# A softmax attention stage on one core: ACT's exponentials of the second pair's first head, moved to the front of the double turn

## The chip, the cores and the metric

The kernel runs on one NeuronCore of a Trainium2 chip. Its engines are TensorE (PE; PEld is its weight load), VectorE (DVE), ScalarE (ACT), GpSimd (POOL) and SyncE (SP, which only issues DMAs here). Each runs its own list of instructions in order, and they meet at semaphores. The metric is the device time of one execution in microseconds, lower being better. Three runs of the kernel before took 1304.85, 1305.89 and 1306.28 us; the median is 1305.89 us.

## The reference

The input x has shape (32, 256, 128), in float32. Six residual blocks follow each other, each on a layer norm of x: three products with a tanh, a linear attention, the tanh block again, a spectral product (folded into one circulant matrix), a causal softmax attention with 16 heads, and the spectral product again. The change touches only the softmax attention:

```python
q = jnp.einsum('qdh,bcd->bhcq', Q, x) * sq
k = jnp.einsum('qdh,bcd->bhcq', K, x) * sq
v = jnp.einsum('vdh,bcd->bhcv', V, x) * sv
att = jnp.einsum('bhcq,bhCq->bhcC', q, k) / d_query
causal = jnp.arange(T)[:, None] >= jnp.arange(T)[None, :]
att = jnp.where(causal, att, -jnp.inf)
p = jax.nn.softmax(att, axis=-1)
y = jnp.einsum('bhcC,bhCv->bhcv', p, v)
z = jnp.einsum('dvh,bhcv->bcd', W, y) * (math.sqrt(d_embed / d_value) / num_heads)
```

## The kernel before

x stays in SBUF for the whole program. Four phases (FFN, linear attention, FFN, spectral) go over 16 groups of two batches. Then comes the softmax stage, from about 267 us to the end: 32 batches, each in 8 turns p = 0 to 7, one turn per pair of heads (n = 8b + p). PE and POOL are written by turns. DVE and ACT are written by double turns: p = 0, 2, 4, 6, each with the pairs n and n+1. Below, "turn 6" of ACT means this double turn. The order on every engine is fixed by the order of the calls in its `batch` function. The first two and the last two batches are written out, the others run in a loop of two.

For a pair, PE computes q and k (`qk_product`, six products into one PSUM bank, L1058 to L1060). ACT copies the bank of an even pair out (`qk_whole`, L749, into `qk_raw`, semaphore `qk_out`), which frees the bank for the next odd pair. ACT then casts the high part (`qk_high_even` L755, `qk_high_odd` L761), and DVE computes the low part (`qk_low`, L506). PE computes the scores of two heads (`scores`, L1073), with those of pairs n+2 and n+3 one behind the other in the odd turn. DVE masks them and takes row maxima (`mask_scores`, L520). ACT takes the exponentials with their sums (`exp_head`, L776, one call per head: a 128x128 and a 128x256 ACTIVATE, each with a read of the sum). DVE inverts the sums (L528), POOL scales (`scale_probs`, L326 and L328, semaphore `pn_ready`), PE transposes (`probs_transpose`, L1087), DVE and ACT copy the transposes to `pT` (L535, L785), and PE multiplies with the values (`products`, L1104). The results of two pairs lie in one bank, from which ACT copies y to the ring `space` (`y_out`, L802, semaphore `y_ready`).

Between these, PE has other work by turn. Turns 0 and 1 hold values of this batch, turn 2 the transposes of x (L1050) and of the spectral part (L1121), turns 3 to 5 the output projection of the last batch (L1113) and the spectral product (L1129), and turns 6 and 7 values of the next batch (L1093 to L1095). ACT copies the values out (`values_out`, L793) in turns 0 and 6.

Three of PE's waits concern what ACT delivers around the change:

```python
pe.wait_ge(exp_ready, count(2 * n - 2))                               # L1067, scores
pe.wait_ge(y_ready, count(y_calls))                                   # L1085, fifth of six transposes
pe.wait_ge(qk_out, count(b * (PAIRS // 2) + (p // 2 + 2)))            # L1159, odd qk_product
```

The first means that the scores of pair n+3 wait until both heads of pair n+1 have gone through the exponential, since they take the same PSUM banks. `X_TURN` is 2, and PAIRS is 8. The buffers `pr` are three: even pairs use buffer 0, odd pairs 1 and 2 in turn.

Of the kernel before, what the change touches and what calls it, by code (L numbers as in the profile page):

```python
# [54 lines left out]
def count(n):  # L55

    return n.i * n.step + n.base if isinstance(n, Count) else n
# [49 lines left out]
def above_0(n):  # L107

    return isinstance(n, Count) or n > 0


def build(nc, x, Wq, bq, Wd, bd, Wu, bu, Wo, bo, W1, W2, W3, ffn_bias, Q, K, V, W, w_re, w_im, fft_bias, dft, out):
    ctx = ExitStack()
    with ctx:
# [128 lines left out]
        X_TURN, LN_TURN, W_TURN, V_TURN, Z_TURN = 2, 4, 3, 6, 6  # L243

        def pr_of(p):

            return 0 if p % 2 == 0 else 1 + p % PAIRS // 2 % 2
# [389 lines left out]
        def _(act):  # L637
# [101 lines left out]
            def x_high(b, j):  # L739
                act.wait_ge(tr_done, count(b + (SOFT + 1)))  # L740
                if above_0(2 * PAIRS * (b - 1)):
                    act.wait_ge(s_done, count(2 * PAIRS * (b - 1)))
                nc.scalar.copy(x_hi[:, j, :], ps[:, BANK_X, 0:T]).then_inc(xhi_ready, 1)

            def qk_whole(n):
                act.wait_ge(qk_done, count(n + 1))
                if above_0(n - 1):
                    act.wait_ge(qklo_ready, count(n - 1))
                nc.scalar.copy(qk_raw[:], ps[:, BANK_QK, :]).then_inc(qk_out, 1)  # L749

            def qk_high_even(n, evens):
                act.wait_ge(qk_out, count(evens))
                if above_0(2 * n - 2):
                    act.wait_ge(s_done, count(2 * n - 2))
                nc.scalar.copy(qk_hi[:, 0].rearrange("p s k -> p (s k)"), qk_raw[:]).then_inc(qkhi_ready, 1)  # L755

            def qk_high_odd(n):
                act.wait_ge(qk_done, count(n + 1))
                if above_0(2 * n - 2):
                    act.wait_ge(s_done, count(2 * n - 2))  # L760
                nc.scalar.copy(qk_hi[:, 1].rearrange("p s k -> p (s k)"), ps[:, BANK_QK, :]).then_inc(qkhi_ready, 1)  # L761

            def exp_head(n, j, h, buf):

                act.wait_ge(max_ready, count(2 * n + (1 + h)))
                if h == 0:
                    kept = n - 1 if buf == 0 else n - 3
                    if above_0(kept):
                        act.wait_ge(pt_done, count(kept))
                    if above_0(n - 1):  # L770
                        act.wait_ge(rinv_ready, count(n - 1))
                for qt in range(2):
                    w = (qt + 1) * P
                    at = 2 * h + qt
                    dst = pr[:, buf, h, 0, :] if qt == 0 else pr[:, buf, h, 1:3, :].rearrange("p b k -> p (b k)")
                    last = nc.scalar.activation(dst, ps[:, BANK_S + 2 * j + h, qt * P:qt * P + w], ACT.Exp,  # L776
                                                bias=neg_max[:, j, at:at + 1], scale=-1.0, accum_out=rsum[:, j, at:at + 1])
                last.then_inc(exp_ready, 1)

            def probs_T(n, j):  # L780

                act.wait_ge(pt_done, count(n + 1))
                if above_0(n - 1):
                    act.wait_ge(pv_done, count(n - 1))
                nc.scalar.copy(pT[:, j].rearrange("p h b q -> p (h b q)")[:, 512:768], ps[:, BANK_Y, j * T:(j + 1) * T]).then_inc(pTb_ready, 1)  # L785

            def values_out(b, j, c, bank=BANK_X):

                act.wait_ge(v_done, count(4 * b + (c + 1)))
                if c == 0:  # L790
                    if above_0(PAIRS * (b - 1)):
                        act.wait_ge(pv_done, count(PAIRS * (b - 1)))
                nc.scalar.copy(vv[:, j, c % 2, 512 * (c // 2):512 * (c // 2) + 512], ps[:, bank, :]).then_inc(v_ready, 1)  # L793

            def y_out(b, jb, p, first=False):

                act.wait_ge(pv_done, count(b * PAIRS + p))
                if p == 1 and above_0(b - 1):
                    act.wait_ge(w_done, count(b - 1))
                at = jb * PAIRS + p - 1  # L800
                if at > 0:
                    nc.scalar.copy(y_ring[:, (at - 1) * T:(at + 1) * T], ps[:, BANK_Y, :]).then_inc(y_ready, 1)  # L802
                else:
                    if not first:
                        nc.scalar.copy(yT[:, 1, PAIRS - 1, :], ps[:, BANK_Y, 0:T])
                    nc.scalar.copy(yT[:, 0, 0, :], ps[:, BANK_Y, T:2 * T]).then_inc(y_ready, 1)
# [5 lines left out]
            def z_xT_out(b, w_after=None):  # L812
                act.wait_ge(z_tr_done, count(b + 1))
                if above_0(b):
                    act.wait_ge(w_done, count(b + 1 if w_after is None else w_after))
                nc.scalar.copy(z_xT[:], ps[:, BANK_X, T:2 * T]).then_inc(z_xT_ready, 1)
# [13 lines left out]
            def batch(b, jb, first=False, last=False):  # L830
                for p in range(0, PAIRS, 2):
                    n = b * PAIRS + p
                    if p > 0:
                        y_out(b, jb, p - 1, first)
                    elif not first:
                        y_out(b - 1, 1 - jb, PAIRS - 1)
                    if not (last and p == PAIRS - 2):
                        qk_whole(n + 2)
                    if p == 0:
                        values_out(b, jb, 2)  # L840
                    if p == X_TURN and above_0(b - 1):
                        z_xT_out(b - 2)
                    if p == X_TURN and not last:
                        x_high(b + 1, 1 - jb)
                    if p == V_TURN and not last:
                        values_out(b + 1, 1 - jb, 0)
                    if not (last and p == PAIRS - 2):
                        qk_high_even(n + 2, b * (PAIRS // 2) + (p // 2 + 2))
                    exp_head(n + 1, 1, 0, pr_of(p + 1))
                    if not (first and p == 0):  # L850
                        probs_T(n - 1, 1)
                    if not (last and p == PAIRS - 2):
                        qk_high_odd(n + 3)
                    exp_head(n + 1, 1, 1, pr_of(p + 1))
                    if p == 0:
                        values_out(b, jb, 3)
                    if p == V_TURN and not last:
                        values_out(b + 1, 1 - jb, 1)
                    probs_T(n, 0)
                    if not (last and p == PAIRS - 2):  # L860
                        exp_head(n + 2, 0, 0, 0)
                        exp_head(n + 2, 0, 1, 0)

            batches(act, batch)
            y_out(B - 1, 1, PAIRS - 1)
            z_xT_out(B - 2)
# [378 lines left out]
```

## Time and profile before

| what | value |
|---|---|
| median of 3 runs | 1305.89 us |
| the profiled execution's own time | 1308.45 us |
| its span (first to last instruction) | 1306.7 us |
| PE matmul busy | 1245.7 us, 95% |
| PE weight load busy | 1072.3 us, 82% |
| DVE busy | 1028.3 us, 79% |
| ACT busy | 1006.9 us, 77% |
| POOL busy | 589.8 us, 45% |
| mean granted TensorE clock | 0.990 |

The busy shares are means over the whole program. The chain that ended last runs over PE for 88% of the span. In a matmul line of the timeline, the distance between two starts tells more than the duration, because matmuls overlap. A wait in brackets names the engine and line that ended it. Waits under 0.17 us are not shown in brackets and have to be read from distances between starts.

### The profile page before, as it was taken

Reading aid. Unit: us, or ns where it says so; the run is one execution under the profiler, and the core shown is the slowest. Engines: PE = TensorE matmul, PEld = TensorE weight load, DVE = VectorE, ACT = ScalarE, POOL = GpSimd, SP = SyncE. Lnnn points to the kernel's source line nnn. Section 1 sums busy time; section 2 is a strip of 40 time slices with the busy share of each in tenths; the row PEclk is TensorE's granted clock in tenths of the full one; section 3 lists DMA queues with packets and bytes.
Section 4 is the critical chain, followed back from the end, with each engine's and each line's share of the span. In section 5 each row is a group of like instructions: output and inputs, shape, how many; then the busy total and the mean of one; then the engine's idle time right before and its main releaser. Section 6 shows DMA issues by size and latency. Waiting matters only on the chain.

```text
span 1306.7 us, 38948 instructions
## 1 busy us (share of the span) xinstructions
PE 1245.7 (95%) x11323; PEld 1072.3 (82%) x11331; DVE 1028.3 (79%) x4813; ACT 1006.9 (77%) x3393; POOL 589.8 (45%) x913
## 2 busy tenths in 40 slices
PE   5799987799999999999999999999999999999997
PEld 4688876778788888888888888888888888888885
DVE  6877779977778787778787878788787878787774
ACT  4744448578788888888888888888888888888883
POOL 5811138634344444444444444444444444444443
PEclk9999989989999999999999999999999999999999
DMA  8000000000000000000000000000000000000000
GB/s 215 1 1 0 1 1 1 1 2 2 3 3 9 8 0 8 0 8 0 8 0 8 0 8 0 8 0 8 0 8 0 8 0 8 0 8 0 9 2 18
DMA packets 14303, 11.83 MB, mean 9 GB/s; under 512 B 709, under 2 KB 12522, under 8 KB 14058
## 3 DMA queue, kind: packets, MB, share of 16 engines
q1 hardware_dynamic: 14240, 11.19, 3.2%
q8 instruction: 24, 0.39, 0.1%
q14 instruction: 29, 0.24, 0.1%
q10 hardware_dynamic: 10, 0.00, 0.0%
HBM read 7.00 MB, written 4.19 MB: 9 GB/s over the span
## 4 chain that ended last, share of the span: by engine, by line
PE 88%; DVE 4%; issue 3%; POOL 2%; ACT 2%; DMA 1%; SPq 1%; DVEq 0%; POOLq 0%; ACTq 0%
PE ps L1073 16%; PE ps L1104 14%; PE ps L1087 13%; PE ps L1113 9%; PE ps L1058 6%; PE ps L1059 5%; PE ps L1060 5%; PE ps L1095 2%; PE ps L1094 2%; PE ps L1093 2%; PE ps L987 2%; PE ps L945 1%; PE ps L1005 1%; PE ps L1035 1%; PE ps L1129 1%
## 5 line engine op out<-in xcount | busy, mean ns | idle before, releaser
L776 ACT ACTIVATE pr<-ps,neg_max 128x128 f32<-128x128 f32 (+1 forms) x1024 | 425.9, 431 | 118.6 <-DVE neg_max L520 118.6
L326 POOL TENSOR_TENSOR pr<-pr,rinv 128x256 f32<-128x256 f32 x256 | 157.9, 617 | 555.9 <-DVE rinv L528 555.9
L520 DVE CUSTOM_DVE_ANT_0 ps<-ps,mask 128x128 f32<-128x128 f32 (+1 forms) x1024 | 329.2, 389 | 3.3
L328 POOL TENSOR_TENSOR pr<-pr,rinv 128x512 f32<-128x512 f32 x256 | 266.6, 1041 | 0.0
L535 DVE COPY pT<-ps 128x512 f32<-128x512 f32 x256 | 175.4, 685 | 100.9 <-PE ps L1087 100.9
L776 ACT ACTIVATION_READ_ACCUMULATOR pr<-ps,neg_max 128x1 f32 x1024 | 219.0, 214 | 0.0
L1087 PE MATMUL ps<-ident,pr 128*128 128x128 f32 x1536 | 210.2, 273 | 2.4 <-POOL pr L328 1.1
L1087 PEld LDWEIGHTS ps<-ident,pr 128*128 128x128 f32 x1536 | 179.1, 141 | 21.4 <-POOL pr L328 2.4
L1104 PE MATMUL ps<-pT,space 128*64 128x256 f32 (+1 forms) x2048 | 194.9, 332 | 0.7 <-ACT pT L785 0.5
L1104 PEld LDWEIGHTS ps<-pT,space 128*64 128x64 f32 x2048 | 126.8, 136 | 55.0 <-ACT pT L785 0.7
L1058 PE MATMUL ps<-x_hi,wqk_hi 128*128 128x256 f32 x512 | 168.1, 328 | 3.0 <-issue 2.6
L1073 PE MATMUL ps<-qk_hi 64*128 64x128 f32 (+1 forms) x1024 | 162.9, 313 | 1.6 <-DVE qk_lo L506 0.5
L1059 PE MATMUL ps<-x_lo,wqk_hi 128*128 128x256 f32 x512 | 144.4, 282 | 0.0
L1060 PE MATMUL ps<-x_hi,wqk_lo 128*128 128x256 f32 x512 | 144.0, 281 | 0.0
L1073 PE MATMUL ps<-qk_lo,qk_hi 64*128 64x128 f32 (+1 forms) x1024 | 143.1, 274 | 0.0
L1073 PE MATMUL ps<-qk_hi,qk_lo 64*128 64x128 f32 (+1 forms) x1024 | 142.7, 274 | 0.0
L520 DVE DVE_READ_ACCUMULATOR2_ANT neg_max<- 128x1 f32 x1024 | 142.0, 139 | 0.0
L1113 PE MATMUL ps<-wz,space 128*128 128x128 f32 x1024 | 132.7, 278 | 0.6 <-ACT space L810 0.6
L506 DVE TENSOR_TENSOR qk_lo<-ps,qk_hi 128x512 fp32r<-128x512 f32 x128 | 88.5, 692 | 51.2 <-ACT qk_hi L761 47.6
L1073 PEld LDWEIGHTS ps<-qk_hi 64*128 64x128 f32 x1024 | 97.7, 186 | 34.8 <-issue 21.1
L1113 PEld LDWEIGHTS ps<-wz,space 128*128 128x128 f32 x1024 | 122.1, 191 | 3.8 <-issue 0.8
L1058 PEld LDWEIGHTS ps<-x_hi,wqk_hi 128*128 128x128 f32 x512 | 96.6, 189 | 26.1 <-issue 24.2
(171 smaller groups left out, 2582.5 us busy)
## 6 DMA issues: line engine op xcount, KB each, us to landing
out<-x_all SPq DMA_DIRECT2D x16, 256.0 KB, 2.3
x_all<-L_attn_x SPq DMA_DIRECT2D x1, 768.0 KB, 6.1
x_all<-L_attn_x SPq DMA_DIRECT2D x1, 512.0 KB, 4.0
space<-L_attn_Q SPq DMA_DIRECT2D x1, 512.0 KB, 15.6
space<-L_attn_K SPq DMA_DIRECT2D x1, 512.0 KB, 9.8
space<-L_attn_V SPq DMA_DIRECT2D x1, 512.0 KB, 11.6
space<-L_attn_W SPq DMA_DIRECT2D x1, 512.0 KB, 11.9
dft_s<-dft SPq DMA_DIRECT2D x1, 192.0 KB, 2.6
```

The source lines that it names most:

```text
L326: nc.gpsimd.tensor_tensor(pr[:, buf, :, 0, :], pr[:, buf, :, 0, :], r[:, :, 0:1].to_broadcast([P, 2, P]), ALU.mult)
L328: nc.gpsimd.tensor_tensor(pr[:, buf, :, 1:3, :].rearrange("p h b k -> p h (b k)"), pr[:, buf, :, 1:3, :].rearrange("p h b k -> p h (b k)") ...
L520: last = nc.vector.tensor_tensor_reduce(o, o, mask[:, T - w:T], -1.0, -MASKED, ALU.add, ALU.min, neg_max[:, j, 2 * h + qt:2 * h + qt + 1])
L535: nc.vector.tensor_copy(pT[:, j].rearrange("p h b q -> p (h b q)")[:, 0:512], ps[:, BANK_T, :]).then_inc(pTa_ready, 1)
L776: last = nc.scalar.activation(dst, ps[:, BANK_S + 2 * j + h, qt * P:qt * P + w], ACT.Exp, bias=neg_max[:, j, at:at + 1], scale=-1.0, accum ...
L1058: mm(o, wqk_hi[:, s, of_pair], x_hi[:, jb, :], start=True, stop=False, skip_group_check=True)
L1059: mm(o, wqk_hi[:, s, of_pair], x_lo[:, jb, :], start=False, stop=False, skip_group_check=True)
L1060: last = mm(o, wqk_lo[:, s, of_pair], x_hi[:, jb, :], start=False, stop=True, skip_group_check=True)
L1073: last = mm(ps[:, BANK_S + 2 * j + h, qt * P:qt * P + w], q[of_head, j, 0, qt * P:(qt + 1) * P], key[of_head, j, 1, 0:w], start=(k == 0), ...
L1087: last = tr(to, pr[:, buf, k // 3, k % 3, :], ident[:])
L1104: last = mm(ps[k * DV:(k + 1) * DV, BANK_Y, half * T + kt * P:(half + 1) * T], vv[:, jb, kt, h * DV:(h + 1) * DV], pT[:, j, k, 0:2, :] if ...
L1113: last = mm(ps[:, BANK_X, t * D:(t + 1) * D], yT[:, j, p, t * P:(t + 1) * P], wz[:, p, :], start=(p == 0), stop=(p == PAIRS - 1), skip_gro ...
```

## The change

In the double turns 0, 4 and 6, ACT calls `exp_head` for the first head of pair n+1 as the first thing of the turn, directly behind the two heads of pair n, which close the turn before. Until now it stood behind the copy of y, the copy of `qk_raw`, the values copy (in turns 0 and 6) and the cast `qk_hi`. In turn 2 it stays there. The second head stays where it was in all turns. No instruction is added or removed.

```diff
             def batch(b, jb, first=False, last=False):
                 for p in range(0, PAIRS, 2):
                     n = b * PAIRS + p
+                    if p != X_TURN:
+                        exp_head(n + 1, 1, 0, pr_of(p + 1))
                     if p > 0:
                         y_out(b, jb, p - 1, first)
                     elif not first:
@@ -846,7 +848,8 @@
                         values_out(b + 1, 1 - jb, 0)
                     if not (last and p == PAIRS - 2):
                         qk_high_even(n + 2, b * (PAIRS // 2) + (p // 2 + 2))
-                    exp_head(n + 1, 1, 0, pr_of(p + 1))
+                    if p == X_TURN:
+                        exp_head(n + 1, 1, 0, pr_of(p + 1))
                     if not (first and p == 0):
                         probs_T(n - 1, 1)
                     if not (last and p == PAIRS - 2):
```

ACT's rows of a turn 6 before the change, up to the second head; `space` in L802 is the ring of y, and in L793 it is the values:

```order
L802 COPY space<-ps 128x512 [waits pv_done]
L749 COPY qk_raw<-ps 128x512 [waits qklo_ready,qk_done]
L793 COPY space<-ps 128x512 [waits v_done]
L755 CAST qk_hi<-qk_raw 128x512 [waits s_done,qk_out]
L776 ACTIVATE pr,rsum<-ps,neg_max 128x128 [waits rinv_ready,pt_done,max_ready]
L776 ACTIVATE pr,rsum<-ps,neg_max 128x256
L785 COPY pT<-ps 128x256 [waits pv_done,pt_done]
L761 CAST qk_hi<-ps 128x512 [waits s_done,qk_done]
L776 ACTIVATE pr,rsum<-ps,neg_max 128x128 [waits max_ready]
```

The same turn of ACT after the change:

```order
L776 ACTIVATE pr,rsum<-ps,neg_max 128x128 [waits rinv_ready,pt_done,max_ready]
L776 ACTIVATE pr,rsum<-ps,neg_max 128x256
L802 COPY space<-ps 128x512 [waits pv_done]
L749 COPY qk_raw<-ps 128x512 [waits qklo_ready,qk_done]
L793 COPY space<-ps 128x512 [waits v_done]
L755 CAST qk_hi<-qk_raw 128x512 [waits s_done,qk_out]
L785 COPY pT<-ps 128x256 [waits pv_done,pt_done]
L761 CAST qk_hi<-ps 128x512 [waits s_done,qk_done]
L776 ACTIVATE pr,rsum<-ps,neg_max 128x128 [waits max_ready]
```

The two ACTIVATEs of the first head have moved in front of four other instructions. L785 and everything behind it has the same work in front of it as before.

In turn 4, which has no values copy, ACT's rows before the change are:

```order
L802 COPY space<-ps 128x512 [waits pv_done]
L749 COPY qk_raw<-ps 128x512 [waits qklo_ready,qk_done]
L755 CAST qk_hi<-qk_raw 128x512 [waits s_done,qk_out]
L776 ACTIVATE pr,rsum<-ps,neg_max 128x128 [waits rinv_ready,pt_done,max_ready]
L776 ACTIVATE pr,rsum<-ps,neg_max 128x256
```

and after it:

```order
L776 ACTIVATE pr,rsum<-ps,neg_max 128x128 [waits rinv_ready,pt_done,max_ready]
L776 ACTIVATE pr,rsum<-ps,neg_max 128x256
L802 COPY space<-ps 128x512 [waits pv_done]
L749 COPY qk_raw<-ps 128x512 [waits qklo_ready,qk_done]
L755 CAST qk_hi<-qk_raw 128x512 [waits s_done,qk_out]
```

Here they pass three instructions. The lists of PE, DVE and POOL are the same before and after.

## Rows read from the trace of the kernel before

**Rows 1.** Window over the softmax stage: us; busy us (instructions) of PE, PEld, DVE, ACT, POOL; clock; DMA
```profile
340.00:1290.00 950.00, 947.21 (x9204) 820.75 (x9204) 757.88 (x3622) 796.61 (x2818) 434.33 (x593) 1.00 0.01 4
```

**Rows 2.** Waits, 340 to 1300 us: who for whom, us in total, times, longest
```profile
PEld ps L1073 <- ACT pr L776: 10.6, 56, 0.3
```

**Rows 3.** Timeline of ACT, turn 6: start, us, instruction, [idle before]
```profile
808.08 0.60 ACT L802 COPY space<-ps 128x512 f32<-128x512 f32 x1
808.75 0.59 ACT L749 COPY qk_raw<-ps 128x512 f32<-128x512 f32 x1
809.44 0.59 ACT L793 COPY space<-ps 128x512 f32<-128x512 f32 x1
809.92 0.63 ACT L755 CAST qk_hi<-qk_raw 128x512 fp32r<-128x512 f32 x1
810.45 0.37 ACT L776 ACTIVATE pr<-ps,neg_max 128x128 f32<-128x128 f32 x1
...
811.25 0.38 ACT L785 COPY pT<-ps 128x256 f32<-128x256 f32 x1
811.50 0.61 ACT L761 CAST qk_hi<-ps 128x512 fp32r<-128x512 f32 x1
...
812.69 0.24 ACT L776 ACTIVATION_READ_ACCUMULATOR pr<-ps,neg_max 128x1 f32 x1
```

**Rows 4.** Timeline of PE, the same turn
```profile
807.73 0.39 PE L1058 MATMUL ps<-x_hi,wqk_hi 128*128 128x256 f32 x1
...
809.24 0.82 PE L1087 MATMUL ps<-ident,pr 128*128 128x128 f32 x6
809.82 0.37 PE L1058 MATMUL ps<-x_hi,wqk_hi 128*128 128x256 f32 x1
...
812.07 0.33 PE L1073 MATMUL ps<-qk_hi 64*128 64x128 f32 x2
...
812.98 0.33 PE L1073 MATMUL ps<-qk_hi 64*128 64x128 f32 x2
```

**Rows 5.** Timeline of PE, turn 2: the scores of the two pairs
```profile
827.75 0.33 PE L1073 MATMUL ps<-qk_hi 64*128 64x128 f32 x2
...
828.54 0.22 PE L1073 MATMUL ps<-qk_hi 64*128 64x128 f32 x2
```

**Rows 6.** Timeline of ACT and PE, turn 0
```profile
815.81 0.60 ACT L802 COPY space<-ps 128x512 f32<-128x512 f32 x1
...
816.33 0.59 ACT L749 COPY qk_raw<-ps 128x512 f32<-128x512 f32 x1
...
817.40 0.36 PE L1058 MATMUL ps<-x_hi,wqk_hi 128*128 128x256 f32 x1
```

**Rows 7.** Timeline of DVE, turns 6, 0 and 2
```profile
807.57 0.14 DVE L520 DVE_READ_ACCUMULATOR2_ANT neg_max<- 128x1 f32 x1
...
810.71 0.68 DVE L506 TENSOR_TENSOR qk_lo<-qk_raw,qk_hi 128x512 fp32r<-128x512 f32 x1
...
813.45 0.29 DVE L520 CUSTOM_DVE_ANT_0 ps<-ps,mask 128x128 f32<-128x128 f32 x1
...
821.02 0.29 DVE L520 CUSTOM_DVE_ANT_0 ps<-ps,mask 128x128 f32<-128x128 f32 x1
...
828.75 0.29 DVE L520 CUSTOM_DVE_ANT_0 ps<-ps,mask 128x128 f32<-128x128 f32 x1
```

**Rows 8.** Timeline of ACT and PE, turn 4
```profile
831.12 0.60 ACT L802 COPY space<-ps 128x512 f32<-128x512 f32 x1
...
833.50 0.37 PE L1058 MATMUL ps<-x_hi,wqk_hi 128*128 128x256 f32 x1
```

**Rows 9.** Timeline of PE, batch 0, turn 0
```profile
276.43 0.39 PE L1058 MATMUL ps<-x_hi,wqk_hi 128*128 128x256 f32 x1 [0.34 <-ACT qk_raw L749]
```

**Rows 10.** Timeline of PE, last batch, turn 6
```profile
1286.50 0.41 PE L1087 MATMUL ps<-ident,pr 128*128 128x128 f32 x2 [0.56 <-ACT space L802]
...
1287.84 0.87 PE L1087 MATMUL ps<-ident,pr 128*128 128x128 f32 x6 [0.93 <-POOL pr L328]
```

## Prediction

> **What bounds the kernel now.** I read the softmax stage first, because the edit touches nothing else. One window over 950 us of it [rows 1] shows the matmul side of TensorE (PE) busy for 947.21 us at a granted clock of 1.00, while ACT is busy for 797 us and VectorE (DVE) for 758 us. So the end of this stage is set by PE's instruction stream. ACT's order matters only at the places where PE waits for ACT.
>
> The Trainium skill, "Perfetto Trace Analysis", section Identifying the Most-Contended Engine, warns against exactly this reading: matmul busy time flatters PE, and the busy share of the weight loads should be taken instead. By that rule PE would stand at 820.75 of 950 us [rows 1], 86%, and would have slack in which neither a later nor an earlier ACT result counts, so the sum below would be zero instead of +8.5 us. The trace does not settle this by a busy share; the distances between starts in [rows 4, 5] speak against the rule here.
>
> The second view is the list of waits. Inside the stage PE waits for ACT in one place that repeats: the weight load of the score products (L1073) waits for `pr` (the exponentials), 56 times, 10.6 us in all [rows 2]. In the timeline each of these is a gap in front of the scores of the *second* pair. In turns 6 and 0 the first pair's scores start at 812.07 and the second's at 812.98, 0.91 us later [rows 4]; in turn 2, where nobody is late, the same distance is 828.54 - 827.75 = 0.79 us [rows 5]. So PE loses 0.12 us per such turn, and what it waits for is the second head of pair n+1: its last read ends at 812.69 + 0.24 = 812.93, and PE starts 0.05 us later [rows 3, 4]. I use this 0.05 us for every hand-over from ACT to PE or DVE. The 56 waits are two in nearly every batch, in turns 6 and 0.
>
> **The change, turn by turn.** Nothing is added or removed. One `exp_head` (two ACTIVATEs with their reads) goes from behind the casts to the front of the turn. Its cost on ACT is read from the same rows: 811.25 - 810.45 = 0.80 us from its start to the start of what follows. So the copies of y, of `qk_raw` and, where they exist, the values copy and `qk_hi` come up to 0.80 us later; from `probs_T` on ACT has done the same work as before. No DMA is issued by ACT in the loop and PE, DVE and POOL keep their order. Two of the late results are wanted by PE: `y_ready` in front of the fifth transpose (L1085), and `qk_out` in front of the odd pair's `qk_product` (L1159).
>
> *Can the exponentials start that early?* In turn 6 ACT is free at 808.08, and DVE's maxima for this head end at 807.57 + 0.14 = 807.71 [rows 3, 7]. Yes, with 0.37 us to spare; so the edit does what it says.
>
> *Turn 6, the new wait.* Exponentials 808.08 to 808.88. The y copy then starts at 808.88 and lasts 0.60, so `y_ready` comes at 808.88 + 0.60 + 0.05 = 809.53. PE's transposes start at 809.24 and take (809.82 - 809.24)/6 = 0.097 each, so the fifth wants it at 809.63: just in time, 0.1 us of slack. One copy behind another starts 0.52 us after it (816.33 - 815.81 [rows 6]), so `qk_raw` starts at 809.40 and ends at 809.99. Before, it started at 808.75, held back by PE, so 0.07 us of the 0.80 is idle time that gets used. PE wants to start the odd `qk_product` at 809.82 [rows 4]; it now starts at 809.99 + 0.05 = 810.04: a wait of 0.22 us, to which I add 0.02 us because the first weight load is then no longer under the transposes (the first product after a wait takes 0.39 instead of 0.37 us, [rows 9] against [rows 4]). **Cost 0.24 us.**
>
> *Turn 6, the old wait.* ACT goes on: values 809.88, `qk_hi` 810.36 (0.48 us after the values copy, as 809.92 - 809.44), `probs_T` 810.89 (0.53 later, as 810.45 - 809.92), odd `qk_hi` 811.14 (0.25 later). Its input arrives 1.02 us after the products start, as in 808.75 - 807.73 [rows 3, 4], that is at 811.06. So it starts 0.36 us earlier than before (811.50) and the second head ends at 812.57. PE's second scores start at 812.07 + 0.24 + 0.79 = 813.10 and no longer wait for it. They would have started at 812.98. **Gain 0.12 us, net +0.12 us.** Here the edit pays 0.24 to get back 0.12.
>
> *DVE in turn 6.* Its first `qk_lo` moves from 810.71 to 810.98 + 0.05 = 811.03, the two normalisations behind it keep their place and their 0.6 us, the second `qk_lo` therefore ends at about 812.8, before PE's 813.10. The `pT` copy and the masks follow at about 813.43, as before (813.45 [rows 7]). So ACT gets its next maxima at the same time as before and turn 0 begins on ACT as in the trace, while PE begins it 0.12 us late.
>
> *Turn 0.* The same sum from 815.81 [rows 6]: exponentials to 816.61, y copy to 817.21, `qk_raw` 817.13 to 817.72, PE starts at 817.77 + 0.02 instead of 817.40, so +0.38 against the trace, of which 0.12 was carried in: cost 0.25 or so. The second head ends well before the scores, so the 0.12 us gap goes again: net +0.12 us. The first scores come 2.25 us after the odd `qk_product` (812.07 - 809.82), at 820.04, and the mask of the next pairs 1.00 us after these, as 828.75 - 827.75 in turn 2 [rows 5, 7]: 821.04, against 821.02 in the trace. ACT's next exponentials are not pushed.
>
> *Turn 2* is not edited. PE comes 0.24 us late, ACT's `qk_raw` waits for PE and is late by the same, and everything moves together. *Turn 4*: the y copy starts at 831.12 [rows 8] and would start at 831.92; `qk_raw` would end at 833.03, and PE wants it at 833.50. The project-out matmuls hide the 0.80 us, and there was no gap to win: zero. If that cover were gone it would cost up to 0.8 us per batch.
>
> **Sum.** 61 steady turns (turn 6 of batches 1 to 30, turn 0 of batches 1 to 31) by 0.12 us: +7.3 us. Batch 0 is leaner on PE: in its turn 0 PE already waits for `qk_raw`, 0.34 us [rows 9], so there the full 0.80 us lands. Part of it is given back at the second scores and part is absorbed while PE waits for DVE in turn 2; I estimate +0.6 us for the batch, between 0 and 1.5. In the last turn 6 PE waits for the y copy, 0.56 us [rows 10]; that copy is 0.80 us later, the transposes' end, the `pT` copies and the last head follow, and the next transposes (1287.84) start some 0.65 us later. Everything after is one chain: +0.65, between 0 and 0.8. Together +8.5 us. The profiled execution took 1308.45 us (span 1306.7), so it would take 1317.0; the shown runs have a median 2.6 us lower, so the same 8.5 us gives **1314.4 us**.
>
> Bounds: the unseen term is the wait for `qk_out` in a busy turn. From the restart cost at nothing and a copy that hands over 0.02 us sooner, 0.08 us net a turn: 61 x 0.08 = 4.9 us and the ends at about 0.6, 1311.4. From one more 0.05 us a turn (the tight `y_ready`, or the masks), 0.17: 10.4 us and the ends at 2.3, 1318.6. I take 0.12, the value the rows give.
>
> **The rivals.**
> 1. *The gap closes and nothing opens: faster.* Place: the second scores in turns 6 and 0. Price: 61 x 0.12 = 7.4 us, so 1298.5. It decides if `qk_raw` is ready before PE's 809.77, that is if ACT's delay stays under 0.43 us. For it: the 10.6 us of waits are real [rows 2], and ACT idles for 153 of 950 us [rows 1]. Against it: that idle time does not lie here; the exponentials, the y copy and `qk_raw` stand back to back in front of PE's wait and end 0.65 us late [rows 3].
> 2. *Hidden: no change.* The new wait is no longer than the old one, or PE has slack that matmul records do not show. Then 0 to +2.6 us, about 1307. For it: both terms are 0.1 to 0.2 us, near the resolution of such sums. Against it: turn 2 shows that without a wait the distance is 0.79 and not 0.91, so PE's stream does respond to 0.12 us.
> 3. *The old gap stays.* DVE's `qk_lo`, 0.3 us later, becomes what the second scores wait for, and 0.24 us a turn is paid in full: 61 x 0.24 + 1.3 = 15.9 us, 1321.8. Against it: it ends at 812.8 and is wanted at 813.05.
>
> **How the numbers follow.** Forecast 0.68, rival 1 0.11, rival 2 0.13, rival 3 0.08. The forecast's own range is 1311.4 to 1318.6. To hold 8 in 10 I reach down through the hidden case and a little above: 1305 to 1319. A change of 0.2%, 2.6 us, is what these runs can tell from none. Faster by more: 0.11. Within: rival 2 and a thin tail of the forecast, 0.14. Slower by more: 0.75.
>
> **What would show it.** In the new profile: PE's odd `qk_product` (L1058 behind L1087) with an idle time of about 0.2 us, released by ACT's `qk_raw`, some 61 times, 10 to 15 us in all; no more waits of L1073 for `pr` in turns 6 and 0, so distances of 0.79 there; batches 0.24 us longer (turns 6 and 0 by 0.12 each, turns 2 and 4 unchanged). Wrong in rival 1's way would be no wait for `qk_raw`; in rival 3's, a wait of L1073 for `qk_lo`; and if turn 4 grew, the cover by project-out was misread.

## The result, and the profile after

Eleven runs of the changed kernel have a median of 1311.18 us, eleven runs of the kernel before taken with them 1306.78 us. The ratio is 1.0028, with a 95% interval of 1.0015 to 1.0041, which is +3.7 us (+2.0 to +5.4). So the change makes the kernel a little slower, in the direction of the forecast, but by less than half of the 8.5 us that were forecast.

The profiled execution took 1311.18 us, its span 1309.4 us. First the window over the softmax stage, to be read against [rows 1], with the same columns: PE is as full as before, and ACT has no more work.

```profile
340.00:1290.00 950.00, 947.74 (x9189) 817.24 (x9188) 761.17 (x3618) 784.66 (x2811) 433.12 (x592) 1.00 0.01 4
```

Then the list of waits of the changed kernel, 340 to 1310 us (who waited for whom, us in total, times, longest). PE's lines have moved down by three, so L1061 is `qk_product` and L1076 the scores.

```profile
PEld ps L1061 <- ACT qk_raw L749: 11.9, 58, 0.2
DVE qk_lo L506 <- ACT qk_hi L755: 9.9, 45, 0.2
```

The wait of the scores for `pr` [rows 2] has gone completely. In its place PE waits for `qk_raw`, 58 times, 11.9 us. This is what the forecast asked for as its sign: some 61 times, 10 to 15 us. DVE, too, now waits for the later cast `qk_hi`; before, that cast (L755) does not stand in the list.

The timeline of PE in a turn 6 after the change, to be read against [rows 4]:

```profile
807.54 0.39 PE L1061 MATMUL ps<-x_hi,wqk_hi 128*128 128x256 f32 x1
...
809.05 0.82 PE L1090 MATMUL ps<-ident,pr 128*128 128x128 f32 x6
809.82 0.39 PE L1061 MATMUL ps<-x_hi,wqk_hi 128*128 128x256 f32 x1
...
812.07 0.33 PE L1076 MATMUL ps<-qk_hi 64*128 64x128 f32 x2
...
812.87 0.23 PE L1076 MATMUL ps<-qk_hi 64*128 64x128 f32 x2
...
813.65 1.52 PE L1107 MATMUL ps<-pT,space 128*64 128x256 f32 x16
...
815.10 0.39 PE L1061 MATMUL ps<-x_hi,wqk_hi 128*128 128x256 f32 x1
...
817.52 0.39 PE L1061 MATMUL ps<-x_hi,wqk_hi 128*128 128x256 f32 x1
...
822.80 0.39 PE L1061 MATMUL ps<-x_hi,wqk_hi 128*128 128x256 f32 x1
```

Subtract the turn's start. The odd `qk_product` starts at 2.28 us, 0.19 later than before (809.82 - 807.73 = 2.09). The second scores start 0.80 us after the first. The products (L1107) start 813.65 - 812.87 = 0.78 us after the second scores. The turn is 7.56 us long, against 7.59 before. The last three rows are the turn 0 that follows: its odd `qk_product` starts at 2.42 us (817.52 - 815.10), against 2.08 before, and it is 7.70 us long (822.80 - 815.10). ACT's part of the turn 6, to be read against [rows 3]:

```profile
807.88 0.38 ACT L776 ACTIVATE pr<-ps,neg_max 128x128 f32<-128x128 f32 x1
...
808.67 0.61 ACT L802 COPY space<-ps 128x512 f32<-128x512 f32 x1
809.13 0.63 ACT L749 COPY qk_raw<-ps 128x512 f32<-128x512 f32 x1
```

The copy of `qk_raw` ends at 809.76, and PE starts 0.06 us later.

The starts of PE's `qk_product`, taken from the timeline for all 32 batches, give the length of every double turn. In the loop they repeat to 0.02 us. Before the change, turns 0 and 2 come in two kinds, in odd and even batches; why, I did not look into. The table has the steady length, and the sums over the program, in us:

| | before | after | difference |
|---|---|---|---|
| turn 6, steady | 7.58 | 7.57 | -0.01 |
| turn 0, steady, odd and even batches | 7.58, 7.66 | 7.70, 7.70 | +0.12, +0.04 |
| turn 2, steady, odd and even batches | 7.88, 7.93 | 7.88, 7.88 | +0.01, -0.04 |
| turn 4, steady | 8.75 | 8.75 | 0 |
| sum of 31 turns 6 | 238.01 | 237.81 | -0.20 |
| sum of 32 turns 0 | 243.27 | 247.14 | +3.87 |
| of these, batch 0 | 6.90 | 7.43 | +0.53 |
| of these, batch 2 | 7.67 | 8.71 | +1.04 |
| sums of turns 2 and 4, but for the last turn 4 | 520.82 | 520.79 | -0.03 |
| of these, turn 2 of batch 30 | 7.87 | 8.13 | +0.26 |
| before the first turn | 274.43 | 271.63 | -2.80 |
| start of the last turn 4 to PE's last instruction | 26.82 | 28.72 | +1.90 |

In turn 2 of batch 30 PE now waits 0.2 us for DVE's `x_lo` (L500), a wait that is not in the list of before.

The 2.80 us ahead of the softmax stage lie in code that the change does not touch. The start of the first turn varied between 270.75 and 275.80 us over the eleven profiles of this study, so this is scatter, and it hides part of the loss in this one execution. Two other entries hold more than the waits: in the turn 0 of batch 2 and at the end PE's clock was low for some us. They come below.

### The profile page after: what moved, and what is told of

It is laid out like the page before. It is cut to its first block, busy times and chain, and to the rows that moved or that the text cites. A ratio compares the mean times of both kernels' runs of the same rounds, so it can differ in the third digit from the quotient of the medians.

```text
span 1309.4 us, 38956 instructions
## 1 busy us (share of the span) xinstructions
PE 1248.0 (95%) x11331; PEld 1069.8 (82%) x11331; DVE 1033.7 (79%) x4813; ACT 995.8 (76%) x3393; POOL 589.2 (45%) x913
## 4 chain that ended last, share of the span: by engine, by line
PE 90%; DVE 3%; issue 3%; ACT 2%; DMA 1%; SPq 1%; POOL 0%; DVEq 0%; POOLq 0%; ACTq 0%
PE ps L1076 15%; PE ps L1107 14%; PE ps L1090 13%; PE ps L1116 9%; PE ps L1061 8%; PE ps L1062 5%; PE ps L1063 5%; PE ps L1098 2%; PE ps L1096 2%; PE ps L1097 2%; PE ps L948 2%; PE ps L970 2%; PE ps L990 2%; PE ps L1008 1%; PE ps L1038 1%
## 5 line engine op out<-in xcount | busy, mean ns | idle before, releaser
L776 ACT ACTIVATION_READ_ACCUMULATOR pr<-ps,neg_max 128x1 f32 x1024 | 222.0, 217 | 0.0
L1090 PE MATMUL ps<-ident,pr 128*128 128x128 f32 x1536 | 213.7, 273 | 3.2 <-ACT space L802 1.9
L1107 PE MATMUL ps<-pT,space 128*64 128x256 f32 (+1 forms) x2048 | 196.1, 334 | 0.7 <-ACT pT L785 0.5
L1061 PE MATMUL ps<-x_hi,wqk_hi 128*128 128x256 f32 x512 | 169.6, 331 | 3.9 <-issue 2.8
L1107 PEld LDWEIGHTS ps<-pT,space 128*64 128x64 f32 x2048 | 127.4, 137 | 55.4 <-ACT pT L785 0.7
L1076 PE MATMUL ps<-qk_hi 64*128 64x128 f32 (+1 forms) x1024 | 157.0, 301 | 0.6 <-DVE qk_lo L506 0.5
L1076 PE MATMUL ps<-qk_lo,qk_hi 64*128 64x128 f32 (+1 forms) x1024 | 143.4, 275 | 0.0
L1076 PE MATMUL ps<-qk_hi,qk_lo 64*128 64x128 f32 (+1 forms) x1024 | 143.2, 274 | 0.0
L1061 PEld LDWEIGHTS ps<-x_hi,wqk_hi 128*128 128x128 f32 x512 | 96.5, 188 | 39.7 <-issue 24.4
L785 ACT COPY pT<-ps 128x256 f32<-128x256 f32 x256 | 104.3, 408 | 24.6 <-PE ps L1090 20.6
L1076 PEld LDWEIGHTS ps<-qk_hi 64*128 64x128 f32 x1024 | 97.7, 186 | 22.5 <-issue 21.1
```

The lines of the kernel that those rows point to most:

```text
L1061: mm(o, wqk_hi[:, s, of_pair], x_hi[:, jb, :], start=True, stop=False, skip_group_check=True)
L1076: last = mm(ps[:, BANK_S + 2 * j + h, qt * P:qt * P + w], q[of_head, j, 0, qt * P:(qt + 1) * P], key[of_head, j, 1, 0:w], start=(k == 0), ...
L1090: last = tr(to, pr[:, buf, k // 3, k % 3, :], ident[:])
L1107: last = mm(ps[k * DV:(k + 1) * DV, BANK_Y, half * T + kt * P:(half + 1) * T], vv[:, jb, kt, h * DV:(h + 1) * DV], pT[:, j, k, 0:2, :] if ...
```

## The experiments

Each edit is shown against the kernel before, unless it says otherwise. "Theory B" in the expectations is the sum of the prediction. "Theory A" was made after the result was seen: the new wait costs what the sum said or a little less, but closing the old gap gives back about 0.23 us a turn, 0.12 in front of the second scores and 0.11 inside them.

**Turn 6 alone.**

```diff
+                    if p in (6,):
+                        exp_head(n + 1, 1, 0, pr_of(p + 1))
...
-                    exp_head(n + 1, 1, 0, pr_of(p + 1))
+                    if p not in (6,):
+                        exp_head(n + 1, 1, 0, pr_of(p + 1))
```

> The first head goes to the front in turn 6 alone. Theory A (the new one): the wait for qk_raw costs about 0.19 us there, and closing the gap before the second scores gives back 0.23 us, 0.12 in front of them and 0.11 inside them, so turn 6 gets 0.02 to 0.04 us shorter than the 7.58 us of before: 31 turns, about -1 us in the stage, but the last turn 6 costs up to 1.9 us at the end, together 0 to +1 us. Theory B (the sum on record): 0.24 against 0.12, turn 6 gets 0.12 us longer, +3.7 us in the stage and +0.65 at the end.

Measured: ratio 1.0013 (1.0004 to 1.0023), +1.7 us. The steady turn 6 is 7.57 us instead of 7.58 and the 31 turns sum to 237.63 us, 0.38 less than before; turn 0 is as before. Theory A holds in the stage: in turn 6 the exchange is even. What is lost sits at the end of the program: from the start of the last turn 4 to PE's last instruction it took 29.64 us in this profile, 2.82 more than before (more on it below).

**Turn 0 alone.** The same edit with `(0,)`.

> The first head goes to the front in turn 0 alone. Theory A: the wait for qk_raw costs 0.34 to 0.37 us, since PE starts this turn on time, and the gap gives back 0.23, so turn 0 gets 0.11 to 0.14 us longer, +3.5 to +4.5 us over 32 turns, and nothing at the end. Theory B would have 0.37 against 0.12, +0.25 us a turn when it isn't preceded by a late turn 6, +7.7 us.

Measured: ratio 1.0021 (1.0012 to 1.0030), +2.7 us. The steady turn 0 is 7.72 to 7.73 us, with the odd `qk_product` at 2.44 us instead of 2.08; the 32 turns sum to 247.88 us, +4.6, of which 1.2 are the one turn in batch 2. The loss of the change is in turn 0.

**Turn 4 alone.** The same edit with `(4,)`.

> The first head goes to the front in turn 4 alone. Both theories: PE is busy with the output projection until long after qk_raw is there and has no gap before the second scores, so turn 4 stays at 8.75 us and the whole at 0 within 1 us; only in batch 0, where there is no projection, turn 4 may cost 0.1 to 0.5 us. A rival: half the cost of the change sits here, +2 us.

Measured: ratio 1.0004 (0.9995 to 1.0013). Steady turn 4 is 8.75 us, as before, and in batch 0 it is 7.25 instead of 7.11. The output projection does hide the 0.80 us, and batch 0, which has none, loses only 0.14. The rival falls.

**The gap by itself.** ACT is given time in front of the second head without anything being put in front of `qk_raw`. In the loop's batches this kernel leaves out most of the values that two of the four copies deliver, so it only measures time.

```diff
-                nc.scalar.copy(vv[:, j, c % 2, 512 * (c // 2):512 * (c // 2) + 512], ps[:, bank, :]).then_inc(v_ready, 1)
+                wv = 64 if (isinstance(b, Count) and c % 2 == 0) else 512
+                nc.scalar.copy(vv[:, j, c % 2, 512 * (c // 2):512 * (c // 2) + wv], ps[:, bank, 0:wv]).then_inc(v_ready, 1)
```

> The kernel before, with ACT's values copy of the first and third part narrowed from 512 to 64 columns in batches 2 to 29 and a little beyond (so most of the values are stale). ACT gets some 0.3 us of lead before the second head in turns 6 and 0, nothing is put in front of qk_raw, and PE's list is the same. It measures the gap by itself. Theory A: 0.23 us a turn, turns 6 and 0 at 7.35 to 7.36 us instead of 7.58, about 56 turns, -13 us. Theory B: 0.12 us a turn, -7 us, with 0.89 us still between the start of the second scores and the products.

Measured: ratio 0.9893 (0.9877 to 0.9909), -14.0 us. Turns 6 are 7.36 us and turns 0 are 7.38 us, both kinds; their sums fall by 6.2 and 6.8 us. PE in one turn 6 of this kernel:

```profile
798.36 0.39 PE L1059 MATMUL ps<-x_hi,wqk_hi 128*128 128x256 f32 x1
...
802.69 0.33 PE L1074 MATMUL ps<-qk_hi 64*128 64x128 f32 x2
802.86 0.28 PE L1074 MATMUL ps<-qk_lo,qk_hi 64*128 64x128 f32 x2
...
803.49 0.22 PE L1074 MATMUL ps<-qk_hi 64*128 64x128 f32 x2
803.55 0.28 PE L1074 MATMUL ps<-qk_lo,qk_hi 64*128 64x128 f32 x2
...
804.27 1.52 PE L1105 MATMUL ps<-pT,space 128*64 128x256 f32 x16
```

The first scores start 4.33 us into the turn (802.69 - 798.36), and before the change it was 4.34 (812.07 - 807.73): up to here nothing is gained. Unbroken, the second scores start 0.80 us after the first, the next matmul 0.06 us after that, and the products 0.78 us after the second scores. Before the change, in a turn with the gap, PE's scores began 0.91 us apart [rows 4] and went on like this, with rows that the prediction passed over:

```profile
813.15 0.27 PE L1073 MATMUL ps<-qk_lo,qk_hi 64*128 64x128 f32 x2
...
813.87 1.52 PE L1104 MATMUL ps<-pT,space 128*64 128x256 f32 x16
```

That is 0.17 us after 812.98 instead of 0.06. From the second scores to the products it was 813.87 - 812.98 = 0.89 us, against 0.78 unbroken. So a wait of 0.12 us costs PE 0.22 us. Theory A is shown for the gap, theory B's 0.12 is refuted.

**Behind `qk_raw`, in turn 0.** Turn 6 as in the change (the lines shown are those of turn 0); in turn 0, the whole first head stands between `qk_raw` and the values copy.

```diff
                         qk_whole(n + 2)
+                    if p in (0,):
+                        exp_head(n + 1, 1, 0, pr_of(p + 1))
```

> Turn 6 as in the change (first head at the front), turn 0 with the first head behind the copy of qk_raw and in front of the values copy. Theory A: in turn 0 qk_raw is on time, there is no wait of PE, and the gap closes: 7.35 us instead of 7.58, -7 us over 31 turns; turn 6 -1 us; the end up to +1.9 us. Together -6 us, about 1301. Theory B: turn 0 -0.12, turn 6 +0.12, no change. A rival to both is that qk_hi, later by up to 0.6 us in turn 0, makes DVE's qk_lo late and the gap stays, with turn 0 at 7.58 or more.

Measured: ratio 0.9993 (0.9983 to 1.0003), no change, and by the two ratios 0.35% less than the changed kernel (4.6 us, give or take 2). Turn 0 is 7.52 and 7.60 us. Theory A had 7.35, and failed by 0.17 to 0.25: the odd `qk_product` is on time at 2.08 us, the scores follow without a gap, but between them PE's second block of transposes comes at 3.75 and 3.83 us instead of 3.57. The list of waits of this kernel, 340 to 1270 us:

```profile
PEld ps L1063 <- ACT qk_raw L749: 5.6, 29, 0.2
PEld ps L1098 <- ACT space L793: 2.3, 13, 0.2
```

L1098 is the second product of values, which waits for the copy of the first. Only 13 of these waits are long enough to be listed, but the later transposes show them in both kinds of turn 0. That is a third deadline, and the prediction's sum did not have it: there PE was late already, for `qk_raw`.

**Only into ACT's idle time.** Between `qk_raw` and the values copy ACT idled some 0.2 us, since it waited for PE's value products. The first ACTIVATE alone (128x128) goes there; `exp_head` gets an argument for it.

```diff
+            def exp_head(n, j, h, buf, parts=(0, 1)):
...
                         qk_whole(n + 2)
+                    if p in (0, 6):
+                        exp_head(n + 1, 1, 0, pr_of(p + 1), (0,))
...
-                    exp_head(n + 1, 1, 0, pr_of(p + 1))
+                    exp_head(n + 1, 1, 0, pr_of(p + 1), (1,) if p in (0, 6) else (0, 1))
```

> In turns 6 and 0 only the first ACTIVATE (128x128) of the first head moves, and only behind the copy of qk_raw, where ACT otherwise idles some 0.2 us until PE's value products are done; its second ACTIVATE stays behind qk_hi. Theory A (PE has three deadlines in such a turn: y, qk_raw, values; ACT must only fill idle time in front of them): all three are kept, the second head is ready 0.2 us earlier, the gap closes, turns 6 and 0 at 7.36 to 7.39 us, -14 us in all, about 1293. If filling the slot weren't enough for the second head (it needs 0.12 us in turn 6, 0.12 or 0.2 in turn 0), some turns would stay at 7.58 or 7.66. Theory B: -0.12 us a turn, -7 us.

Measured: ratio 0.9917 (0.9903 to 0.9930), median 1297.0 us, -10.9 us: faster than both kernels. ACT in a turn 6 of this kernel, which PE began at 800.86:

```profile
801.21 0.60 ACT L804 COPY space<-ps 128x512 f32<-128x512 f32 x1
801.88 0.59 ACT L749 COPY qk_raw<-ps 128x512 f32<-128x512 f32 x1
802.36 0.37 ACT L777 ACTIVATE pr<-ps,neg_max 128x128 f32<-128x128 f32 x1
802.72 0.59 ACT L795 COPY space<-ps 128x512 f32<-128x512 f32 x1
803.18 0.64 ACT L755 CAST qk_hi<-qk_raw 128x512 fp32r<-128x512 f32 x1
803.70 0.49 ACT L777 ACTIVATE pr<-ps,neg_max 128x256 f32<-128x256 f32 x1
```

`qk_raw` starts 1.02 us into the turn, as before, and the cast 2.32 us, against 2.19 before. The ACTIVATE holds up the values copy by 0.36 us (802.72 - 802.36), yet that copy starts only 0.15 us later in the turn than before (1.86 us against 809.44 - 807.73 = 1.71), so 0.21 us of it went into idle time. Turns 6 are 7.38 us, one kind of turn 0 is 7.37; the other is 7.52, where filling the slot was not enough to close the larger gap (its second scores start 0.87 us after the first). This accounts for some 2 us of the 3 that are missing to -14. The list of waits has no wait of PE for ACT left in the loop; what is left is too short to be listed.

**Half in front, half behind `qk_raw`.**

```diff
+                    if p in (0, 6):
+                        exp_head(n + 1, 1, 0, pr_of(p + 1), (0,))
                     if p > 0:
                         y_out(b, jb, p - 1, first)
...
                         qk_whole(n + 2)
+                    if p in (0, 6):
+                        exp_head(n + 1, 1, 0, pr_of(p + 1), (1,))
```

> In turns 6 and 0 the first ACTIVATE of the first head goes to the front of the turn, the second behind the copy of qk_raw. Theory A: y and qk_raw just make their deadlines (1.87 and 2.01 us after PE's start of the turn against 2.03), the values copy ends at 2.8 against 2.8 in turn 6 and 0.1 late in turn 0; turn 6 about 7.38 us, turn 0 about 7.45, together -10 us. If the deadlines were 0.1 us tighter than I read them, turns 6 and 0 would be at 7.5 and 7.55, -4 us.

Measured: ratio 0.9968 (0.9956 to 0.9980), -4.2 us. `y` and `qk_raw` keep their deadlines (odd `qk_product` at 2.08 us in both turns). Turn 0 is 7.52 us, with PE's second block of transposes at 3.75 us, as when the head stood behind `qk_raw`: the values are late. Turn 6 is 7.55 us, not 7.38, and there another deadline is missed. DVE and PE of one turn 6:

```profile
746.49 0.68 DVE L506 TENSOR_TENSOR qk_lo<-ps,qk_hi 128x512 fp32r<-128x512 f32 x1
```

```profile
747.31 0.33 PE L1080 MATMUL ps<-qk_hi 64*128 64x128 f32 x2
```

The second scores start 0.14 us after this `qk_lo` ends (747.17). It is late because the cast of the even pair is, and two normalisations stand between the two `qk_lo`. The -4 us that the expectation named for tighter deadlines came out, but in turn 6 for another reason than it gave.

**One place earlier only.** The whole head in front of the cast `qk_hi`, behind the values copy, in turns 6 and 0.

```diff
+                    if p in (0, 6):
+                        exp_head(n + 1, 1, 0, pr_of(p + 1))
                     if not (last and p == PAIRS - 2):
                         qk_high_even(n + 2, b * (PAIRS // 2) + (p // 2 + 2))
```

> In turns 6 and 0 the whole first head moves only one place, from behind the cast qk_hi to in front of it and behind the values copy. Theory A: no idle time of ACT lies between these two, so ACT fills nothing, the second head is ready when it was, the gap stays: turns 6 at 7.58, turns 0 at 7.58 and 7.66 us, change within 1 us. Only the cast is 0.8 us later; if DVE's qk_lo, which waits for it, then becomes what the second scores wait for, turn 6 (where two normalisations stand between the two qk_lo) gets 0.1 to 0.4 us longer, up to +12 us. Rival: that the exponentials come earlier is itself of use (POOL and DVE get them sooner), then a few us faster.

Measured: ratio 1.0071 (1.0058 to 1.0085), +9.3 us. Turn 0 stays at 7.58 and 7.66; turn 6 is 7.92 us, +0.34. Of this, 0.14 lie ahead of the first scores, which start 4.47 us into the turn instead of 4.33; the rest lies at the second. DVE, and then PE's weight load, in one turn 6 (start 746.68):

```profile
750.33 0.69 DVE L506 TENSOR_TENSOR qk_lo<-qk_raw,qk_hi 128x512 fp32r<-128x512 f32 x1 [0.59 <-ACT qk_hi L755]
750.94 0.59 DVE L420 TENSOR_SCALAR xn<-x_all,mv,rstd 128x128 f32 x2
751.45 0.68 DVE L506 TENSOR_TENSOR qk_lo<-ps,qk_hi 128x512 fp32r<-128x512 f32 x1
```

```profile
752.26 0.19 PEld L1076 LDWEIGHTS ps<-qk_hi 64*128 64x128 f32 x2 [0.36 <-ACT pr L776]
```

The profile names ACT as the releaser, but ACT's last ACTIVATE of that head (751.28, 0.51 us) had ended at 751.79. The other half of PE's wait, `qk_lo`, ended at 752.13, and PE went on 0.13 us later. So it came as the expectation's second case had it. This is the rival "the old gap stays" of the prediction, reached by another order. The rival of this expectation, that early exponentials are of use by themselves, falls.

**The end of the program.** Against the changed kernel:

```diff
-                    if p != X_TURN:
+                    if p != X_TURN and not (last and p == PAIRS - 2):
                         exp_head(n + 1, 1, 0, pr_of(p + 1))
```

> The changed kernel, but in the last batch's turn 6 the first head keeps its old place. Theory A: in the end of the changed kernel PE waits 1.36 us for the y copy instead of 0.56, and its clock then falls to half for some 3 us; both go, the time from the start of the last double turn to the end returns from 28.7 to 26.8 us, -1.9 us, and the rest is as in the changed kernel. Rival: the low clock comes by itself in some executions; then the low stretch stays and only the 0.7 us of waiting goes.

Measured: ratio 1.0026 (1.0009 to 1.0043) against the kernel before, so +3.4 us, which can't be told from the change's +3.7. The end itself, from the start of the last turn 4 to PE's last instruction, took 26.92 us, as before. In the changed kernel it took 28.72, and this is its window there (columns as in [rows 1]; the eighth is PE's clock):

```profile
1286.00:1290.00 4.00, 1.76 (x15) 1.22 (x12) 2.27 (x15) 3.19 (x14) 2.46 (x4) 1.00 0.00 0
...
1291.00:1292.00 1.00, 1.00 (x10) 0.75 (x8) 0.87 (x4) 0.00 (x0) 0.83 (x2) 0.50 0.00 0
1292.00:1293.00 1.00, 1.00 (x10) 0.64 (x6) 0.00 (x0) 0.00 (x0) 0.79 (x1) 0.50 0.00 0
```

After 4 us in which PE was busy for 1.76 us, its granted clock fell to 0.50, the lower of its two levels (1.2 GHz), for some 3 us. Other profiles take this apart. With turn 0 alone moved, PE waits only 0.57 us for the last y copy and yet had the low clock, with an end of 28.0 us. In the kernel "behind `qk_raw`" PE waits 1.36 us, as in the changed kernel, and is busy for the same 1.76 of 4 us, at full clock, and its end took 27.78 us. With turn 6 alone moved, PE waits 1.36 us too, had the low clock for some 6 us, and its end took 29.64 us. So the late copy costs at most 1.0 us (27.78 against 26.82; two kernels without a later y copy had 27.06, so some 0.2 of it may be scatter), and the low clock another 1 to 2 us when it comes. It came in two of the three profiles with the 1.36 us wait, and in one of the eight others. Whether the longer wait makes it more likely stays open, and with it the expectation's theory that both go together.

## Why the prediction was wrong

**The mechanism was right.** The exponentials start at the turn's front, since their maxima are there. `qk_raw` ends late, PE waits for it once in turns 6 and 0, the waits for `pr` vanish, turn 4 does not change and turn 2 hardly, and the whole gets slower. Rival 1 (nothing opens) is refuted by the 58 waits. Rival 2 (hidden) is refuted in turn 0 of the odd batches; in turn 6, and over turns 0 and 2 of the even batches together, its number is the right one, for another reason: two effects of equal size. Its 0 to +2.6 us and the measured +3.7 (2.0 to 5.4) overlap, so it is the lengths of the turns that decide, not the total. Rival 3 did not occur here.

**The step that failed is the worth of the old gap**: "So PE loses 0.12 us per such turn" and, from it, "Gain 0.12 us, net +0.12 us". I took the distance between the first and the second scores and stopped there. The block behind the wait is itself 0.11 us longer, and a distance that ended at the products would have held both. The narrowed values copy measured the whole gap at 0.22 us in turn 6 and 0.20 to 0.28 in turn 0 (two kinds; the prediction took the smaller for all). The terms side by side, in us a turn:

| | forecast | measured |
|---|---|---|
| wait for `qk_raw`, turn 6 | 0.24 | 0.20 |
| gap given back, turn 6 | 0.12 | 0.21 |
| wait for `qk_raw`, turn 0 | 0.25 beyond a 0.12 carried in | 0.33, nothing carried in |
| gap given back, turn 0 | 0.12 | 0.21 and 0.29 |
| turn 2 | 0 | +0.01 and -0.04 |
| net of a batch | +0.24 | +0.12 (odd) and -0.02 (even), so +0.05 |

The measured waits are the mean shifts of the odd `qk_product`, from 2.08 to 2.28 us in turn 6 and from 2.08 to 2.41 us in turn 0 (0.19 in the turn shown); what is given back follows from them and the turns' lengths.

**The sum again.** 30 steady batches by 0.05 are 1.5 us instead of 7.3. Batch 0 cost 0.53 + 0.07 + 0.12 - 0.03 = 0.7 (forecast 0.6), the end 0.7 to 1.0 without the low clock (forecast 0.65), and the wait for `x_lo` in batch 30, which the forecast did not have, 0.3. Together 3.2 to 3.5 us, and the ratio says 3.7 (2.0 to 5.4). The two smaller terms were sized right, the large one nearly five times too large.

The wait itself was some 0.05 us shorter than forecast in turn 6. ACT's copies follow each other after 0.46 us (809.13 - 808.67) when no input is awaited, not after the 0.52 that I took from turn 0, and against that the copy takes 0.63 us, not 0.59. The 0.02 us that I added for the first weight load did not show either: from the odd `qk_product` to the first scores it is 812.07 - 809.82 = 2.25 us, before and after. And where the prediction says that 0.07 us of the 0.80 is idle time that gets used, its own numbers give 0.15 (0.80 less 809.40 - 808.75 = 0.65); the sum used the 0.65.

**On the rule about the busy share.** The weight loads' busy share after the change is 86% again. With that slack PE's turns still got 0.2 us shorter when the gap was closed, and 0.34 us longer when `qk_lo` was late (the whole head in front of the cast): the turn's length followed PE's waits in every experiment. The Trainium skill, "Perfetto Trace Analysis", section Identifying the Most-Contended Engine, says to judge TensorE's headroom by that share and by the share of its peak rate; it does not say that such headroom hides a wait, which was the prediction's reading, and here it did not.

## What to carry to other kernels

A wait on a saturated engine is worth the change in the distance from a point ahead of it to a point well behind it, measured against an unbroken instance of the same work, not the length of the hole. When an instruction of an in-order helper engine is moved, list every result that it passes with the time at which somebody wants it (here y, `qk_raw`, the values, `qk_hi`); the piece may only be as long as the idle time in front of each of them plus the slack that it still has. Splitting the head and putting only its first part into the idle slot turned +3.7 us into -10.9.

## What the runs showed of the hardware

- Score matmuls on 64 rows: where they follow other scores without a break, the second scores' first matmuls are followed after 0.06 us, after a wait of PE only after 0.17 us, and the whole block takes 0.89 instead of 0.78 us. The first scores, which stand behind transposes, have the 0.17 us without any wait for data (802.86 - 802.69): what a wait loses is the run from one block of scores into the next. The full-height `qk_product` loses next to nothing behind a wait (2.25 us to the first scores, with it and without).
- From the recorded end of ACT's copy or exponential to PE's start it is 0.05 to 0.06 us (812.93 to 812.98, 809.76 to 809.82), from the end of DVE's `qk_lo` 0.13 to 0.14 us (752.13 to 752.26, 747.17 to 747.31).
- At the entry of PE's loop, all eleven profiles show an idle time of 1.15 to 2.78 us that waits for nothing the profile shows. Behind it the granted clock fell in some: in the changed kernel it was 0.55 and 0.60 in the two halves of the 4 us from 335, and the turn 0 of batch 2 took 8.71 us instead of the steady 7.70. Of the profiles, the changed kernel and five others (turn 0 alone, behind `qk_raw`, into the idle time, one place earlier, the end) have this long turn, the kernel before and four others do not. All six of the first group move the first head or a part of it ahead in turn 0, but so does one of the second (half in front, half behind). So it may be a further price of the change of about 1 us, by the clock; no run settles it.
